# Aggregating a graph layer with two split products and picked rows for the remainders

## What is computed

```python
m = jax.nn.relu(x[src]) + EPS
z = m * t
e = jnp.exp(z - zmax[dst])
denom = jax.ops.segment_sum(e, dst, num_segments=N)
alpha = e / (denom[dst] + 1e-16)
agg = jax.ops.segment_sum(alpha * m, dst, num_segments=N)
h = agg + x
h = jax.nn.relu(_ln(h @ w1 + b1, lg, lb))
return h @ w2 + b2
```

## Time and profile before

| | before |
|---|---|
| median of 3 runs | 955.58 us (955.27 to 955.77) |
| the profiled execution | 954.13 us |
| its span | 952.3 us |
| TensorE busy | 885.2 us, 93% |
| VectorE busy | 682.4 us, 72% |
| ScalarE busy | 497.4 us, 52% |
| GpSimd busy | 380.4 us, 40% |
| mean granted clock of TensorE | 0.978 |

### The profile page before, as it was taken

The page is one execution under the profiler, slowest core; times in us unless marked ns, Lnnn a source line. Parts: engine busy times, 40 slices in busy tenths (PEclk is TensorE's granted clock), DMA queues, the critical chain, the costliest instruction groups (busy, mean ns, idle before and its releaser), DMA issues. The chain is left out here.

```text
span 952.3 us, 14446 instructions
## 1 busy us (share of the span) xinstructions
PE 885.2 (93%) x4761; PEld 684.2 (72%) x4761; DVE 682.4 (72%) x1145; ACT 497.4 (52%) x866; POOL 380.4 (40%) x326
## 2 busy tenths in 40 slices
PE   4999898999999999899999898999999999999970
PEld 3898798878877788677888786666666666666640
DVE  5966899866447667777668686687766766776765
ACT  2566499735426354262543235566566566566530
POOL 2002100365005531055310255666666666666630
PEclk9999999999999999999999799999999999999995
DMA  6333100332011220121201714799999999999778
GB/s 183 135 122 122 44 1 2 129 126 89 0 55 55 79 89 1 54 80 60 67 11 56 253 49 177 241 323 352 337 325 366 327 334 365 355 347 331 273 184 210
DMA packets 57165, 159.78 MB, mean 168 GB/s; under 512 B 13901, under 2 KB 21651, under 8 KB 48656
## 3 DMA queue, kind: packets, MB, share of 16 engines
q1 hardware_dynamic: 44725, 147.50, 44.8%
q0 software_dynamic: 12288, 11.36, 4.2%
q10 hardware_dynamic: 91, 0.13, 0.1%
HBM read 152.71 MB, written 25.58 MB: 187 GB/s over the span
## 5 line engine op out<-in xcount | busy, mean ns | idle before, releaser
L263 PE MATMUL ps<-split_operands 128*125 128x512 f32 (+5 forms) x690 | 266.1, 386 | 10.7 <-DVE split_operands L1363 4.6
L265 PE MATMUL ps<-split_operands 128*125 128x512 f32 (+5 forms) x690 | 259.9, 377 | 0.0
L264 PE MATMUL ps<-split_operands 128*125 128x512 f32 (+5 forms) x690 | 259.8, 377 | 0.0
L683 POOL DMA_INDIRECT yrow_scratch<-work,row_i x64 | 151.0, 2359 | 96.1 <-ACT work L1026 93.6
L263 PEld LDWEIGHTS ps<-split_operands 128*125 128x125 f32 (+3 forms) x690 | 129.4, 187 | 40.3 <-DVE split_operands L1363 5.3
L265 PEld LDWEIGHTS ps<-split_operands 128*125 128x125 f32 (+3 forms) x690 | 129.1, 187 | 26.4
L1588 DVE TENSOR_TENSOR gate_up_lo<-expert_weights,split_operands 128x2048 fp32r<-128x2048 f32 x64 | 146.2, 2284 | 0.5 <-ACT split_operands L1008 0.5
L264 PEld LDWEIGHTS ps<-split_operands 128*125 128x125 f32 (+3 forms) x690 | 129.6, 188 | 23.5
L395 POOL TENSOR_TENSOR split_operands<-work,split_operands 128x512 fp32r<-128x512 f32 x66 | 84.0, 1301 | 136.4 <-ACT split_operands L377 124.0
L1008 ACT ACTIVATE split_operands<-expert_weights 128x2048 fp32r<-128x2048 f32 x64 | 121.8, 1903 | 0.0
L2076 PE MATMUL ps<-expert_weights,work 128*117 128x512 f32 x256 | 120.3, 592 | 0.5 <-issue 0.5
(11 more groups left out here) (213 smaller groups left out, 1269.6 us busy)
## 6 DMA issues: line engine op xcount, KB each, us to landing
expert_weights<-experts_in SPq DMA_DIRECT2D x64, 1024.0 KB
expert_weights<-experts_in SPq DMA_DIRECT2D x64, 512.0 KB, 8.0
work<-w_in SPq DMA_DIRECT2D x12, 1024.0 KB, 5.1
yrow_scratch<-work SPq DMA_DIRECT2D x5, 1500.0 KB
split_operands<-yrow_scratch SPq DMA_DIRECT2D x4, 1120.0 KB
work<-cw_in SPq DMA_DIRECT2D x3, 1024.0 KB, 5.1
work<-rows_in SPq DMA_DIRECT2D x10, 256.0 KB, 4.8
work<-wmix_in SPq DMA_DIRECT2D x4, 512.0 KB, 4.9
```

Of the source, the lines that this page charges most:

```text
L263: pe.matmul(o, a[1], b[0], start=start, stop=False)
L264: pe.matmul(o, a[0], b[1], start=False, stop=False)
L265: return pe.matmul(o, a[0], b[0], start=False, stop=stop)
L683: pool.indirect_dma_start(yrow, bass.IndirectOffsetOnAxis(ap=row_i[:, e:e + 1], axis=0), OS[e % 4], None, bounds_check=last_row, oob_is_er ...
```

## The change

Counts up to 2048 are exact in the high part of A as the change takes it, so only a source with more than `MANY` = 2048 edges can have a remainder in `AT_lo`; with 20,625 edges at most `SLOTS` = 10 sources have so many. Each source tile gets 10 slots, 50 in all (`PICKED`). What changes:

- `aggregate` issues four products with `AT_hi` alone (`mm2`), not six.
- GpSimd sums the edges of each source from the running sums (`degree`) and marks the sources with more than 2048 (`many`); TensorE ranks them in their tile (`sources_before`); VectorE builds the 0/1 selector (`select`, five operations of 125 x 50).
- In each layer, in the middle of destination tiles 0 and 1, TensorE picks the marked rows of the high parts of E and E m (`pick`, 10 products), and ScalarE copies them to `ES`. In layer 0 TensorE also picks the remainders of those sources (`remainders`, 10 products of 314 and 312 columns), and ScalarE copies them to `REST` and the selector to `SEL_rest`.
- `add_remainders(d)` adds `REST` x `ES` to each destination tile: two products.
- ScalarE's order: first half of w1, these copies, second half of w1, denominators. In layer 0 the copies wait for the last `adj_low`, since `REST` lies where `AT_lo` was.
- GpSimd's order: `add_x(0)` in the middle of the second half of w1, `add_x(1)` behind it, then all of cw.
- VectorE: `select` (layer 0) or the `cw_add` of tile 3 (layers 1 and 2) moves ahead of the message of source tile 3.
- TensorE: `h_tr(0)` stood before destination tile 3 and `h_tr(1)` before tile 4; now they stand before tile 4 and behind it. The first products of layer 0 wait for `adj_hi`, not `adj_lo`.
- `adj_copy` and the first weight load of SP wait for `degree` too.

```diff
+MANY = 2048
+SLOTS = EDGES // (MANY + 1)
+PICKED = NT * SLOTS
+MARK = 512
+REST_HALVES = [(0, 314), (313, 312)]
...
+        def mm2(o, a, b, start, stop):
+
+            pe.matmul(o, a, b[1], start=start, stop=False)
+            return pe.matmul(o, a, b[0], start=False, stop=stop)
+
...
             sp.wait_ge(S("adj_diff"), NT)
+            sp.wait_ge(S("degree"), NT)
             r = 3 * D
...
+            pool.wait_ge(S("ranges"), 1)
+            g1(pool.memset(before_tile, 1.0))
+            g1(pool.affine_select(out=before_tile, in_=before_tile, compare_op=ALU.is_gt, fill=0.0, base=0,
+                                  pattern=[[1, T + 1]], channel_multiplier=-1))
+            g1(pool.affine_select(out=before_tile, in_=before_tile, compare_op=ALU.not_equal, fill=float(MARK), base=0,
+                                  pattern=[[1, T + 1]], channel_multiplier=-1))
+            pool.wait_ge(S("e_lo"), 2)
+            g1(pool.iota(slot_i, pattern=[[1, PICKED]], base=MARK, channel_multiplier=0))
+            pool.tensor_copy(slot, slot_i)
+            for j in range(NT):
+                pool.wait_ge(S("adj_sb"), j + 1)
+                g1(pool.tensor_tensor(degree_tile if j else degree, cum[j % 2][:, :, T], cum[j % 2][:, :, 0], ALU.subtract))
+                pool.sem_inc(S("degree"), 1)
+                if j:
+                    g1(pool.tensor_tensor(degree, degree, degree_tile, ALU.add))
+            pool.tensor_scalar(many[:, 0:NT], degree, float(MANY), None, ALU.is_gt).then_inc(S("many"), 1)
+
...
-                for nme in (f"w1_{L}0", f"w1_{L}1"):
-                    for c in range(4):
-                        split_lo_part(nme, c, 4)
+                for c in range(4):
+                    split_lo_part(f"w1_{L}0", c, 4)
+                for c in range(2):
+                    split_lo_part(f"w1_{L}1", c, 4)
                 add_x(0)
-                for c in range(2):
-                    split_lo_part(f"cw_{L}", c, 4)
+                for c in range(2, 4):
+                    split_lo_part(f"w1_{L}1", c, 4)
                 add_x(1)
-                for c in range(2, 4):
+                for c in range(4):
                     split_lo_part(f"cw_{L}", c, 4)
...
                     act.wait_ge(S("adj_diff"), j - 1)
+                    act.wait_ge(S("degree"), j - 1)
                 act.activation(cum[j % 2][:, 0:4, :], ps[0:T, 2 * (j % 2), 0:4 * (T + 1)].rearrange("p (s n) -> p s n", s=4),
...
                         exponential_hi(L, s)
-                for nme in (f"w1_{L}0", f"w1_{L}1"):
-                    split_hi(nme)
+                split_hi(f"w1_{L}0")
+                act.wait_ge(S("picked_ps"), L + 1)
+                if not L:
+                    act.wait_ge(S("adj_lo"), NT)
+                for i in range(2):
+                    last = act.activation(ES[:, i, :], ps[0:PICKED, 4 + i, :], ACT.Copy)
+                last.then_inc(S("picked"), 1)
+                if not L:
+                    act.wait_ge(S("rest_ps"), 1)
+                    for h, (n0, nn) in enumerate(REST_HALVES):
+                        last = act.activation(REST[:, cut(n0 + h, nn - h)], ps[0:PICKED, 6 + h, h:nn], ACT.Copy)
+                    last.then_inc(S("rest"), 1)
+                    act.activation(SEL_rest, f(SEL_first), ACT.Copy).then_inc(S("rest"), 1)
+                split_hi(f"w1_{L}1")
...
+            def select():
+
+                dve.wait_ge(S("rank_ps"), 1)
+                for s in range(NT):
+                    last = dve.tensor_scalar(SEL_first[:, s, :], slot, float(-SLOTS * s), ps[0:T, 5, s:s + 1], ALU.add, ALU.is_equal)
+                last.then_inc(S("select"), 1)
+
...
                 for s in range(0 if L else 2, NT + 1):
+                    if s == 3:
+                        if L:
+                            cw_add(L - 1, NT - 2)
+                        else:
+                            select()
                     if s < NT:
...
                 if L:
-                    cw_add(L - 1, NT - 2)
                     cw_add(L - 1, NT - 1)
...
                     b = AGG_BANK[d]
-                    a = (AT_hi[:, s, cut(d * T, T)], AT_lo[:, s, cut(d * T, T)])
-                    mm3(ps[0:T, b, :], a, sub(EX, A_, s, A_), s == 0, s == NT - 1)
-                    last = mm3(ps[0:T, b + 1, :], a, sub(EM, A_, s, A_), s == 0, s == NT - 1)
-                    if s == NT - 1:
-                        last.then_inc(S("agg_ps"), 1)
+                    a = AT_hi[:, s, cut(d * T, T)]
+                    mm2(ps[0:T, b, :], a, sub(EX, A_, s, A_), s == 0, False)
+                    mm2(ps[0:T, b + 1, :], a, sub(EM, A_, s, A_), s == 0, False)
+
+                def sources_before():
+                    pe.wait_ge(S("many"), 1)
+                    pe.matmul(ps[0:T, 5, 0:NT], before_tile[:, 0:T], many[:, 0:NT], start=True, stop=True).then_inc(S("rank_ps"), 1)
+
+                def pick():
+
+                    if L:
+                        pe.wait_ge(S("cw_add"), NT * L - 1)
+                        pe.wait_ge(S("w2_sb"), NT * L - 1)
+                        pe.wait_ge(S("rest"), 2)
+                    else:
+                        pe.wait_ge(S("select"), 1)
+                    for i, v in enumerate((EX, EM)):
+                        for s in range(NT):
+                            last = pe.matmul(ps[0:PICKED, 4 + i, :], (SEL_rest if L else SEL_first)[:, s, :], v[0][:, s, :],
+                                             start=s == 0, stop=s == NT - 1)
+                    last.then_inc(S("picked_ps"), 1)
+
+                def remainders():
+
+                    pe.wait_ge(S("adj_lo"), NT)
+                    for h, (n0, nn) in enumerate(REST_HALVES):
+                        for s in range(NT):
+                            last = pe.matmul(ps[0:PICKED, 6 + h, 0:nn], SEL_first[:, s, :], AT_lo[:, s, cut(n0, nn)],
+                                             start=s == 0, stop=s == NT - 1)
+                    last.then_inc(S("rest_ps"), 1)
+
+                def add_remainders(d):
+
+                    pe.wait_ge(S("picked"), L + 1)
+                    pe.wait_ge(S("rest"), 1)
+                    for i in range(2):
+                        last = pe.matmul(ps[0:T, AGG_BANK[d] + i, :], REST[:, cut(d * T, T)], ES[:, i, :], start=False, stop=True)
+                    last.then_inc(S("agg_ps"), 1)
...
                     if not L and not s:
-                        pe.wait_ge(S("adj_lo"), d + 1)
+                        pe.wait_ge(S("adj_hi"), d + 1)
                         pe.wait_ge(S("adj_sb"), NT if d == 0 else NT - 1)
                     aggregate(d, s)
+                    if not L and (s, d) == (1, 0):
+                        sources_before()
+                    if (s, d) == (4, 0):
+                        pick()
+                    if not L and (s, d) == (3, 1):
+                        remainders()
+                for d in range(2):
+                    add_remainders(d)
                 if L:
...
                     if not L:
-                        pe.wait_ge(S("adj_lo"), d + 1)
+                        pe.wait_ge(S("adj_hi"), d + 1)
                     if d >= 3:
-                        h_tr(d - 3)
                         pe.wait_ge(S("quot"), NT * L + d - 2)
+                    if d == NT - 1:
+                        h_tr(0)
                     for s in range(NT):
...
-
+                    add_remainders(d)
+
+                h_tr(1)
                 weights(f"w1_{L}1")
```

11 lines of the change are left out of this document (added).

## The result

Before 955.67 us (median of 4 runs, 955.27 to 958.79), after **946.50 us** (4 runs, 945.64 to 947.80); ratio 0.9896, 95% interval 0.9879 to 0.9913. The forecast was 946.3 us, range 943.5 to 951.4. The profiled execution of after took 946.22 us with a span of 944.3 us, against 954.13 and 952.3.

The account below looks back on a forecast made before the run. TensorE was taken to bound the kernel before, with VectorE's quotients last after the change. Layer gains 0.0 + 4.7 + 4.6 = 9.3 us, from a median of 955.6, gave 946.3 us; range 943.5 to 951.4.

Parts of the forecast that it names:

- TensorE bounds before, VectorE has room: Aggregation before the change: TensorE busy 39.4 of 40 us in layer 0; VectorE idles between tiles.
- Picking products 0.2325 us apart: Picking products with 50 stationary columns, absent from the trace: taken at 0.2325 us each, bounds 0.147 and 0.43.
- Layer 1, 4.7 us: Layer 1: `times_w1(0)` starts at 320.6 instead of 325.3, set by VectorE's fourth quotient; gain 4.7 us, not 7.0.
- Layer 2, 4.6 us: Layer 2: same chain as layer 1 from a start at 407.14; `times_w1(0)` at 438.3 instead of 442.94, gain 4.6 us.
- Layer 0, 0.0 us: Layer 0: input waits and a later first quotient use up the saving; `times_w1(0)` at 209.75 against 209.72, gain 0.0 us.
- TensorE waits 1.7, 1.5 and 1.5 us: Ahead of `times_w1(0)`: TensorE arrives before VectorE's fourth quotient and waits 1.7 us in layer 0, 1.5 in layers 1 and 2.
- rival (a): TensorE stays last in every layer, so all 19.4 us count, giving 936.2 us; chance 5%.
- Rival (b), the clock: TensorE's clock falls after the new waits, up to 3.0 us each: 949.3 us with one fall, 952.3 with two; chance 10%.
- the prediction's own list: Signs of error: GpSimd or w2-load wait behind `times_w1(0)`, clock under 1 at 170-450 us, picks not 0.2325 apart, unslipped first reciprocal.
- The side sum of 7.8 us: With the skill page's 131 ns per product, 30 products are 3.9 us, TensorE last in layers 1 and 2: 7.8 us.
- The moves that cost nothing: GpSimd's degree work, earlier `add_x(0)`, later cw split and w2 load (1 us of cover), SP's new wait: no cost.
- The expert part keeps its length: Expert part, 600 to 900 us, TensorE busy 299.8 of 300: same length, giving back nothing of the gain.

Follow-up runs that it names:

- no remainders: The change without selection, picked rows, remainders and their copies, keeping only the two split products of the high half and the moved transposes; 943.18 us, 0.986 to before.
- padded rows: The change with 125 slots (75 stay zero), first w1 product in banks 6 and 7, denominators ahead of the second w1 split; 943.02 us, 0.988 to before.
- denominators first: The change with ScalarE's split of the second half of w1 behind denominator(0) and denominator(1) instead of ahead of them; 944.53 us, 0.989 to before.
- long quotient: The change with one more VectorE pass over the denominator, times one, in each quotient; 961.66 us, 1.008 to before.
- long quotient in before: The kernel before with one more VectorE pass over the denominator, times one, in each quotient; 959.23 us, 1.005 to before.
- short quotient: The change with the reciprocal (3.35 us) replaced by a pass that multiplies by zero and adds a constant; 948.98 us, 0.993 to before.
- transposes alone: The kernel before with only the first two transposes of aggregated rows moved one destination tile later; 955.97 us, 1.000 to before.
- full rows: The change with the remainder-adding products taking 125 (wrong) rows instead of 50, same count and columns; 944.43 us, 0.985 to before.

## Why the prediction was right, step by step

- **TensorE bounds before, VectorE has room.** Right. A longer quotient leaves L0 and L1 of before within 0.2 us of where they are. That VectorE had room behind `times_w1(0)` too was only half true, by 1.1 us a layer.
- **Picking products 0.2325 us apart.** Right: ten of them from 297.25 to 299.56. The 50 stationary columns left the spacing as it was; the 50 rows of the pair didn't.
- **Layer 1, 4.7 us.** Measured 4.81. The chain from first reciprocal to fourth product is 16.68 us (said: 16.65), and the first reciprocal 14.10 us behind the aggregation's start (said: 14.2), through the very queue of the prediction: pick, two copies, 1.90 us of w1 split, denominator.
- **Layer 2, 4.6 us.** Measured 4.20 in the first profile, whose layer begins at half clock, and 4.81 in the one without that.
- **Layer 0, 0.0 us.** Measured 0.15, -0.46 and 0.14; the middle one is the profile in which the clock fell there. In the first profile the input waits came as said (2.66 for 2.7, 0.72 for 0.85), `select` took 0.89 for 0.7, the first reciprocal came at 192.41 for 192.9.
- **TensorE waits 1.7, 1.5 and 1.5 us.** Wrong: 0.50, 0 and 0. The step that failed is the end of TensorE's tiles, "302.8 + 3 x 5.12 + 0.25 + 2 x 0.35". A tile takes 5.50, not 5.12 (319.52 less 302.62, less 0.41 for transposes, is three tiles of 5.50), because the pair of 50-row products was costed like its neighbours. The prediction gave the 50 stationary columns of the pick a range and never asked about the 50 rows of the pair. The sum didn't suffer since VectorE was last or level anyway. It would have with a faster VectorE: rival (a), 19.4 us, had no 0.37 us a tile in it.
- **Rival (a), all 19.4 us.** Refuted. Even with the reciprocal gone L1 is 33.66, and with both engines relieved 32.25, a gain of 6.4 against the 7.0 of the count.
- **Rival (b), the clock.** It was real, and more likely and cheaper than said. At the new waits nothing fell in the first profile (0.50, 2.66 and 0.72 us long). In the second it fell behind the 2.66, as in six of the ten profiles with that wait, which the change brought. The price was 0.6 us and not up to 3.0: TensorE had 0.72 us of waiting ahead of source tile 4, which the slower products took up. The clock also fell where the prediction had taken its evidence against it, at the wait of 3.28 us at the start of layer 2: the row of 399 to 404 us shows 0.66, and L2 is 0.6 us longer than in the profile without a fall. By the prediction's own list that was a sign against it; its price was small.
- **The side sum of 7.8 us.** Its reasoning fails by itself: with products closer together than 0.2325 us VectorE, at 3.99 us a quotient, would be last more surely, not TensorE. The forecast doesn't use it.
- **The moves that cost nothing.** Right for GpSimd (order put back, no difference) and for the late w2 load: no wait for either stands behind `times_w1(0)`. The load of cw, of which the prediction says only that its split comes later, is nearly on the path (no remainders, above).
- **The expert part keeps its length.** Not quite: 358.9 us before, 360.1 after. Among the 14 profiles it is 357.1 to 361.1. The three with 10 us or more of waits of ScalarE for expert weights have 360.1, 360.7 and 361.1, the ones without average 358.9. Piece of the chain that ended last, change:

```profile
840.69 20.06 DMA expert_weights<-experts_in
860.78 1.92 ACT split_operands L1061
```

  The DMA share is 0.95 and 0.96 in this part in the two kernels, and the engines are fed at 331 and 337 GB/s, so a little disturbance shows. That an earlier start causes it isn't shown: of the kernels that start earliest (no remainders, padded rows, denominators first) none has such a wait.

That the total met the forecast within 0.2 us is partly luck. The terms were right within 0.5 us each, but the part behind the last layer alone scatters by more. The span of the profiled execution fell by 8.0 us, not 9.3, and the medians by 9.2, 6.1 and 8.1 us in the three comparisons of the change with before.

## What to carry to other kernels

After a cut, look for two engines that end together, and test each by making it longer and shorter by itself. The one that costs when longer but gives nothing when shorter has a partner right behind it, and only a change to both pays. A reordering that is worth next to nothing before a cut can carry more than half of its gain; measure it on the kernel that has the cut.

When a matmul is added, compare its contraction rows with its neighbours' and not only its columns. Filling up to their count with zeros cost TensorE nothing here; in layer 0 VectorE's `select` took 1.09 us instead of 0.89 for it, and ScalarE's copy of the selector 0.73 instead of 0.40.

When the head of a chain is moved forward, ask for each later link what stands ahead of it in its engine's order. Here it was a load behind which the third denominator had to wait.

## What was not expected of the hardware

**Contraction rows.** A pair of 50-row products among 125-row ones costs 0.37 us more than a pair with 125 rows (0.10 ahead, 0.18 over it, 0.09 behind). The ten picking products (125 rows, 50 columns) cost nothing extra. Why, no run shows.

**A pass with more than one price.** The same pass of VectorE over 125 x 512 took 0.43 us or 0.84 to 0.86 in the long quotient, and up to 1.43 in the long quotient in before; the pass of the short quotient took 0.42 to 1.56. Timelines of VectorE and of GpSimd, long quotient, layer 1:

```profile
313.23 0.43 DVE L1451 TENSOR_SCALAR work<-work 125x512 f32<-125x512 f32 x1
...
317.68 0.86 DVE L1451 TENSOR_SCALAR work<-work 125x512 f32<-125x512 f32 x1
```

```profile
309.32 2.55 POOL L416 TENSOR_TENSOR split_operands<-work,split_operands 128x512 fp32r<-128x512 f32 x2 [0.80 <-ACT split_operands L398]
314.46 1.29 POOL L644 TENSOR_TENSOR work<-work,x_cur 125x512 f32<-125x512 f32 x1 [2.60 <-DVE work L1452]
315.71 2.54 POOL L416 TENSOR_TENSOR split_operands<-work,split_operands 128x512 fp32r<-128x512 f32 x2
```

In these rows it is 0.43 while GpSimd idles (311.9 to 314.5) and 0.86 while it works; the reciprocal, 3.35 us, is the same in both. The Trainium skill, "GPSIMD Engine Reference", section "Specifications", says that GpSimd and VectorE share their SBUF interfaces and that VectorE instructions in a two-port mode contend; by "VectorE: DVE Perf Modes", section "Mode 2×_2P — use both read ports for one tensor", this pass is such an instruction. The traces agree: in the three kernels whose quotients have such a pass it takes 0.42 or 0.43 us whenever GpSimd idles, and 0.43 to 1.56 us where the two overlap. GpSimd can pay as well: beside a pass that took only 0.47 us (long quotient in before, 309.99) two of its pieces took 2.72 us instead of 2.54.

**The clock behind a wait.** The wait at the start of layer 2 is 3.15 to 3.44 us in 14 profiles and there in every kernel. Behind it the granted clock of the next 8 us was 1.00 in four of them, 0.79 in four and 0.61 to 0.64 in six. Kernels with the products of before (transposes alone, long quotient in before) are among the falls and the change is once among the profiles without one, so the change didn't bring these. It did bring the wait of 2.66 us in layer 0: of ten profiles with it (2.66 or 2.67 us; 2.87 with padded rows) six show 0.79 over the next 8 us and four 1.00, and of the change's own three one fell. Waits of 2.74 and 2.55 us in the long quotient and of 3.37, 3.37 and 2.55 us without remainders were followed by a fall, one of 2.50 us was not, and none of 1.18 to 1.25 us with full rows. From the last `times_w1(0)` to the first expert product it takes 145.5 to 153.8 us, at granted clocks of 0.98 down to 0.87 between 505 and 600 us; this is where single runs of one kernel part by several us. What decides a single case, no run here shows.
